# Reciprocal softmax row sums carried to all partitions by two DMAs through HBM, in an attention and expert-routing kernel on one Trainium2 core

## What is computed

```python
q = x @ Wq + bq; k = x @ Wk + bk; v = x @ Wv + bv
scores = einsum('bdsh,bdth->bdst', q, k) / SCALE
weights = softmax(scores, axis=-1)
feats = einsum('bdst,bdth->bdsh', weights, v)
x = layernorm(x + feats @ Wo + bo)
```

## Time and profile before

| | |
|---|---|
| device time, median of 3 runs | 1293.24 us (1292.84 to 1294.88) |
| span of the profiled execution | 1289.5 us |
| busy, share of the span | PE 97%, DVE 77%, ACT 71%, POOL 40% |
| attention heads | about 161 to 939 us of the span |
| granted TensorE clock | 0.999 on the mean |

### The profile page before, as it was taken

The page is one execution under the profiler, slowest core; times in us unless marked ns, Lnnn a source line. Parts: engine busy times, 40 slices in busy tenths (PEclk is TensorE's granted clock), DMA queues, the critical chain, the costliest instruction groups (busy, mean ns, idle before and its releaser), DMA issues. The chain is left out here.

```text
span 1289.5 us, 24161 instructions
## 1 busy us (share of the span) xinstructions
PE 1255.7 (97%) x8128; PEld 1058.8 (82%) x8128; DVE 998.2 (77%) x1891; ACT 919.8 (71%) x1643; POOL 513.2 (40%) x508
## 2 busy tenths in 40 slices
PE   7999999999999999999999999999988999999896
PEld 5888799889889889989989989989866877777642
DVE  5623688789889979979979979979866777776387
ACT  5421589778878868868868868878833877778343
POOL 0002223234524524524533533542543666676412
PEclk9999999999999999999999999999999999999999
DMA  8788466212424424323423423543578999997698
GB/s 282 258 283 289 155 196 223 69 42 84 147 66 138 145 70 139 125 88 110 146 84 101 155 89 88 156 136 120 178 272 326 386 386 385 346 339 252 237 426 335
DMA packets 90951, 253.14 MB, mean 196 GB/s; under 512 B 16824, under 2 KB 39480, under 8 KB 87504
## 3 DMA queue, kind: packets, MB, share of 16 engines
q1 hardware_dynamic: 70608, 196.78, 44.9%
q0 software_dynamic: 17920, 50.62, 10.2%
q10 hardware_dynamic: 2304, 4.20, 0.8%
HBM read 177.87 MB, written 134.91 MB: 243 GB/s over the span
## 5 line engine op out<-in xcount | busy, mean ns | idle before, releaser
L967 ACT ACTIVATE p_hi<-slot 128x512 fp32r<-128x512 f32 x512 | 278.5, 596 | 108.9 <-PE slot L1594 105.5
L807 POOL TENSOR_TENSOR p_lo<-prob,p_hi 128x512 fp32r<-128x512 f32 x128 | 166.1, 1297 | 441.9 <-ACT prob L969 441.7
L1607 PE MATMUL slot<-k_stack,q_stack 128*128 128x512 f32 x1024 | 300.1, 415 | 0.0
L984 ACT ACTIVATE prob<-prob,row_min 128x1024 f32<-128x1024 f32 x256 | 296.8, 1160 | 0.1
L1307 DVE TENSOR_TENSOR p_lo<-slot,p_hi 128x512 fp32r<-128x512 f32 x384 | 250.8, 681 | 52.5 <-ACT p_hi L967 51.1
L1594 PE MATMUL slot<-ident,prob 128*128 128x128 f32 x2048 | 265.8, 273 | 1.3 <-ACT prob L984 1.3
L1632 PE MATMUL pv_acc<-p_hi,v_pair 128*128 128x256 f32 x1024 | 263.1, 290 | 2.6 <-POOL p_lo L807 1.8
L1632 PE MATMUL pv_acc<-p_lo,v_pair 128*128 128x256 f32 x1024 | 253.7, 281 | 0.0
L1594 PEld LDWEIGHTS slot<-ident,prob 128*128 128x128 f32 x2048 | 229.5, 141 | 1.9 <-issue 1.7
L1632 PEld LDWEIGHTS pv_acc<-p_hi,v_pair 128*128 128x128 f32 x1024 | 192.6, 188 | 16.1 <-issue 5.7
L1632 PEld LDWEIGHTS pv_acc<-p_lo,v_pair 128*128 128x128 f32 x1024 | 192.8, 188 | 12.9 <-issue 3.3
(11 more groups left out here) (196 smaller groups left out, 1974.4 us busy)
## 6 DMA issues: line engine op xcount, KB each, us to landing
disp_hbm<-zero_hbm SPq DMA_DIRECT2D x64, 518.0 KB, 6.3
rows_all<-disp_hbm SPq DMA_DIRECT2D x64, 518.0 KB, 12.8
y_hbm<-zero_hbm SPq DMA_DIRECT2D x48, 512.0 KB, 4.4
got<-y_hbm SPq DMA_DIRECT2D x15, 1536.0 KB, 19.0
q_stack<-q_hbm SPq DMA_DIRECT2D x128, 128.0 KB, 3.1
up_pair<-in_L_ffn_w_up SPq DMA_DIRECT2D x26, 512.0 KB, 9.5
down_w<-in_L_ffn_w_down SPq DMA_DIRECT2D x32, 256.0 KB, 12.0
q_hbm<-q_hi SPq DMA_DIRECT2D x8, 512.0 KB, 2.7
```

The lines of the kernel that those rows point to most:

```text
L807: e.tensor_tensor(p_lo[1][:, 2:4, :], prob[:, m % 2, :, (4 * u + 2) * P:(4 * u + 4) * P], p_hi[1][:, 2:4, :].bitcast(F32), ALU.subtract).t ...
L967: e.activation(p_hi[b][:, two, :], view[:, two, :], ACT.Copy).then_inc(a_phi, 1)
L984: e.activation(keys, keys, ACT.Exp, bias=row_min[:, me % 2, j, 1:2], scale=-1.0, accum_out=row_sum[:, me % 2, j, half:half + 1]).then_inc( ...
L1607: made = e.matmul(slot[:, n * BANK:(n + 1) * BANK], qs[:, part, j * P:(j + 1) * P], k_stack[:, ms % H, keys], start=part == 0, stop=part == 1)
```

## The change

The two PE transposes per head and the ACT copy go, with their semaphores and the entry in the list of readers of `misc`. SP stores `row_inv` to a small HBM buffer (`store_inverse`, ahead of `load_q`), and two issue steps later loads it back to all 128 partitions of a new buffer `inv_all` (`spread_inverse`). DVE's multiply reads `inv_all` with a stride of two elements and waits for that load. Each DVE row sum waits for the store of the head before. The zeroing is regrouped: three 518 KB pieces a head instead of four, two of them between the store and the load and one behind the load; the 512 KB pieces move from the step before the load's to behind the load. The DMA scratch is set to 8192 bytes a partition.

```diff
+        inv_hbm = hbm("inv_hbm", (2, P, QT))
...
+        inv_all = sb("inv_all", [P, QC], F32, att)
...
+            def store_inverse(m):
+                e.wait_ge(v_inv, m + 1)
+                if m >= 2:
+                    e.wait_ge(d_spread, 16 * (m - 1))
+                e.dma_start(inv_hbm[m % 2], row_inv[:, :]).then_inc(d_inv, 16)
+
+            def spread_inverse(m):
+                e.wait_ge(d_inv, 16 * (m + 1))
+                if m:
+                    e.wait_ge(v_scaled, m)
+                else:
+                    e.wait_ge(v_vlo, NS)
+                    e.wait_ge(g_vlo, NS)
+                    e.wait_ge(a_vhi, 2 * NS)
+                e.dma_start(inv_all[:, :], inv_hbm[m % 2].rearrange("p j -> (p j)").partition_broadcast(P)).then_inc(
+                    d_spread, 16)
+
             jobs = []
             for s in range(LAST + LAG + 2):
+                m, u = divmod(s - LAG, STEPS)
+                if 0 <= m < NCH * H and u == 1:
+                    store_inverse(m)
+                elif 0 <= m < NCH * H and u == 3:
+                    spread_inverse(m)
                 if s < LAST and s % STEPS == STEPS - 1 and s // STEPS + 2 < NCH * H:
                     load_q(s // STEPS + 2)
...
-                elif 2 * STEPS <= s < 2 * STEPS + E - Z_EARLY:
-                    zero_disp(range(Z_EARLY + s - 2 * STEPS, Z_EARLY + s - 2 * STEPS + 1))
-                elif s % 4 == 0 and E <= s < E + 4 * NZ:
-                    e.dma_start(y_pieces[(s - E) // 4], zero_hbm[:, 0:2 * C]).then_inc(d_yzero, 16)
+                elif s >= 2 * STEPS and s % STEPS < 2:
+                    first = Z_EARLY + 3 * (s // STEPS - 2) + 2 * (s % STEPS)
+                    zero_disp(range(first, min(first + 2 - s % STEPS, E)))
+                if s % STEPS == 1 and E <= s < E + STEPS * NZ:
+                    e.dma_start(y_pieces[(s - E) // STEPS], zero_hbm[:, 0:2 * C]).then_inc(d_yzero, 16)
...
-                if 0 <= r < LAST and u == 3:
-                    e.wait_ge(p_spread, m + 1)
-                    if m:
-                        head_out(e, m - 1)
-                    e.activation(scaled[:, :], misc[:, 0:QC], ACT.Copy).then_inc(a_spread, 1)
...
-                    e.wait_ge(a_spread, mv + 1)
+                    e.wait_ge(d_spread, 16 * (mv + 1))
                     e.wait_ge(p_pv, 4 * mv + 4)
                     if mv:
                         head_out(e, mv - 1)
-                    e.tensor_tensor(scaled[:, :], pv_acc[:, 0:QC], scaled[:, :], ALU.mult).then_inc(v_scaled, 1)
+                    e.tensor_tensor(scaled[:, :].rearrange("d (j p) -> d j p", j=QT), pv_acc[:, 0:QC].rearrange("d (j p) -> d j p", j=QT),
+                                    inv_all[:, :].rearrange("d (p j) -> d j p", j=QT), ALU.mult).then_inc(v_scaled, 1)
...
                     e.wait_ge(a_exp, 4 * m + 4)
+                    if m:
+                        e.wait_ge(d_inv, 16 * m)
...
-                if 0 <= r < LAST and u == 3:
-                    e.wait_ge(v_inv, m + 1)
-                    wait_misc()
-                    for j in range(QT):
-                        made = e.transpose(misc[:, j * P:(j + 1) * P], row_inv[:, j:j + 1].to_broadcast([P, P]),
-                                           ident[:, :])
-                    made.then_inc(p_spread, 1)
-                    misc_read.append((a_spread, m + 1))
...
-    nc = _bacc.Bacc("TRN2", target_bir_lowering=False, num_devices=1)
+    nc = _bacc.Bacc("TRN2", target_bir_lowering=False, num_devices=1, dynamic_dma_scratch_size=8192)
```

More of the change, by code:

```diff
@@ L216, in build @@
         p_k, p_q, p_v = (sem(f"pe_{n}") for n in ("k", "q", "v"))
-        p_scores, p_turned, p_pv, p_spread = (sem(f"pe_{n}") for n in ("scores", "turned", "pv", "spread"))
+        p_scores, p_turned, p_pv = (sem(f"pe_{n}") for n in ("scores", "turned", "pv"))
         p_proj, p_x1t, p_gate, p_rank = (sem(f"pe_{n}") for n in ("proj", "x1_turned", "gate", "rank"))
@@ L220, in build @@
         a_xhi, a_whi, a_khi, a_qhi, a_vhi = (sem(f"act_{n}") for n in ("x_hi", "w_hi", "k_hi", "q_hi", "v_hi"))
-        a_exp, a_phi, a_copy, a_spread = (sem(f"act_{n}") for n in ("exp", "p_hi", "p_copy", "spread"))
+        a_exp, a_phi, a_copy = (sem(f"act_{n}") for n in ("exp", "p_hi", "p_copy"))
         a_x1t, a_score = sem("act_x1_turned"), sem("act_score")
@@ L238, in build @@
         d_moved, d_feats, d_st, d_st_late = (sem(f"dma_{n}") for n in ("moved", "feats", "x1_store", "x1_store_late"))
+        d_inv, d_spread = sem("dma_inverse_store"), sem("dma_inverse_spread")
         d_scat = [sem(f"dma_scatter{j}") for j in range(2)]
```

## The result

The changed kernel takes 1409.8 us (median of 4 runs, 1405.2 to 1412.6) against 1293.0 for the kernel before, 9.0% slower (ratio 1.090, 95% interval 1.0877 to 1.0923). The forecast was 1289.4 us in a range of 1280 to 1299. The profiled execution took 1412.6, its span is 1410.5, 121.0 us more than before.

The account below looks back on a forecast made before the run. The prediction took PE's instruction list to bound attention; -14.1 - 0.7 + 8.4 + 1.6 + 1.0 = -3.8 us took the span from 1289.5 to 1285.7, and the median from 1293.2 to 1289.4 us, range 1280 to 1299.

Parts of the forecast that it names:

- What the transposes cost: PE in attention: the two transposes add 0.22 us to each of 64 heads, so removing them gains 14.1 us.
- The strided multiply: DVE's multiply: taken at an unchanged 424 ns; any extra, at most 27 us in 64 heads, hidden behind DVE's idle time.
- round trip: Store and load of the reciprocals: spread lands at T + 5.4, 1.5 us inside DVE's need, costing nothing in plain heads.
- T: The end of a head's reciprocal on DVE, from which the prediction counts its times.
- The allowance: Plain heads: DVE waits for nothing if the spread lands by T + 6.93; PE stalls only from T + 8.07.
- Rival 3: Every head: the round trip is late, spread at T + 9.5, 69 us over 48 heads, 1358 us; chance 0.08.
- the main line: The forecast itself: plain heads free, chunk ends, zeroing heads and last chunk paying a little, 1289.4 us; chance 0.64.
- Chunk ends: Output projection at 7 chunk ends: feats lands late behind store and query loads, PE idle 1.2 us each, 8.4 us.
- rival 1: Chunk ends: the feats stall eats the gain, 26.5 us in 7 stalls, 1307.5 us, deciding from 1.74 us each; chance 0.13.
- The order inside the queue: DMA queue at chunk ends: feats would follow the second query load, stall about 1.5 us, sum 2.0 us worse, 1291.4.
- Zeroing heads: Heads 0 to 7: two 518 KB pieces ahead of the load make it some 0.2 us late each, 1.6 us.
- Last chunk: Residual rows and the shared expert's weights between a store and its load: at most one late head, 1.0 us.

Follow-up runs that it names:

- e14: Changed kernel with reciprocals through one SBUF partition, loaded to 64 partitions, multiplied later by POOL, query loads behind feats, chunk's first projection half a step later: 1289.7 us.
- e1: Kernel before with only the regrouped zeroing and the 8 KB DMA scratch, spread left on PE and ACT: 1292.8 us.
- e15: Changed kernel with the store's 8 B rows 64 B apart in HBM, load from 128 different rows, reciprocal values left out: 1310.1 us.
- e2: Changed kernel with the load filling inv_all from 128 different 1 KB rows of a zeroed buffer, reciprocal values left out: 1377.3 us.
- e3: As e2, and the load does not wait for the store to land; the store is still issued: 1368.1 us.
- e11: Changed kernel with e7_order's SP order; DVE copies the product without waiting, POOL multiplies by the reciprocals after the join, on 64 partitions: 1355.0 us.
- e7_order: Changed kernel with another SP order: load ahead of query loads and zeroing, feats right behind the store: 1366.9 us.
- e17_tuned: e14 with four of POOL's six chunk-end scatters half a step later and the shared expert's weights two steps later: 1286.2 us.
- e13: Changed kernel with reciprocals through one SBUF partition, loaded to 64 partitions, multiplied by POOL after the join, query loads right behind feats: 1298.0 us.
- e10: Changed kernel with the reciprocals going through one SBUF partition instead of HBM, order and waits unchanged: 1397.4 us.

## Why the prediction was wrong

**What the transposes cost: right.** 0.22 us a head was forecast; 0.21 is what unstalled heads gain (11.22 to 11.01 in e14, 15.1 to 14.9 in the changed kernel itself). The strided multiply takes 424 ns as assumed, and the scratch costs nothing (e1; the scatters wait 86.1 us where it was 87.2).

**The step that failed** is the round trip's: "its landing at T + 5.4", and from it "In plain heads the round trip costs nothing." It took 2.0 us for the store from a store of 2 KB rows and 3.1 us for the load from the query loads. Measured: 3.76 and 5.0, the load issued at T + 3.2 in the head shown and not at T + 2.35, since it now waits for the store and not for SP's list, and a landing at T + 8.5 (median). Both rows had the right direction, and the load's the right size, but another shape: the store's rows lie 8 B apart in HBM (e15), the load's 128 reads share one kilobyte (e2). The plain heads, priced at nothing, lost 33.1 us in 30 and 22.3 in the 6 last of a chunk, net of the missing transposes. The allowance was too wide as well: by the prediction PE stalls only from T + 8.07 on. In the 30 heads the spread lands at T + 8.3 (median), hardly later, but each lost 1.1 us. The prediction looked at the multiply alone; DVE's wait also holds up what PE needs of DVE, ACT and POOL afterwards: in the rows of these 30 heads PE stands 6.1 us for the multiply and 15.2 for the `p_lo` of POOL and DVE.

**Rival 3** was the case, at a chance of 0.08: its sign, DVE waiting for a DMA, shows in 46 of 64 heads, and its bounds, 4.6 and 4.8 us, were on the table. It gave 48 heads 69 us; by the table the 49 heads from the second of a chunk on lost some 64. That these agree is in part luck, since the spread landed at T + 8.5 and not T + 9.5. Its 1358 us was too low because it left zeroing heads and chunk ends at the forecast's prices. What it had in common with the main line was to take the store's harm as its own landing only. The runs showed that the transfers behind it are late too (e3, e11): `feats`, `moved` and the query loads.

**Chunk ends**: 8.4 us forecast, 25.8 measured. The mechanism was rival 1's, `feats` behind the store and the query loads: at these 7 ends it lands in 4.6 us (median; 2.6 to 6.3) and not 2.15, the longest beyond the 4.6 of the upper bound. PE stands there for 18.0 us in all, at six of the ends, 2.6 on the mean of 7, and rival 1 decides from 1.74; the multiply and the slower clock cost time there too. The order inside the queue that the prediction weighed pointed the right way, and its 1.5 us a stall were still too few. **Zeroing heads**: 1.6 us forecast, 27.0 measured in seven. With the load moved ahead of the zeroing they take 85.0 us in e7_order (summed as in the table) and not 105.6, so the order is most of it. **Last chunk**: 1.0 forecast, 10.5 measured in its last six heads; the one late head that was priced took 4.7 us of it.

**Not in the sum at all: the clock.** e17_tuned and the changed kernel issue the same 8000 PE instructions:

```profile
PE 1242.5 (97%) x8000; PEld 1045.5 (82%) x8000; DVE 1003.1 (78%) x1891; ACT 901.8 (70%) x1579; POOL 562.2 (44%) x572
```

PE is busy for 1290.8 us in the one and 1242.5 in the other, 48.3 us more for the same list, at a mean clock of 0.971 and 0.996. The spans differ by 127.7 us (1410.5 and 1282.8); the other 79.4 are idle time. So to each microsecond for which PE stood came on the mean 0.6 us more of busy time. The clock makes up at most 36 of the 48 us: 0.029 of 1410.5 us less 0.004 of 1282.8. Where the rest comes from was not tried.

Open: whether the scatters could move without making PE wait at the chunk ends, and whether rows 16 or 32 B apart with a wider load would do; neither was tried.

## What to carry to other kernels

Price a new transfer by a row of the same shape, not of the same size: here the landing hung on how many pieces went to, or came from, one place in memory, and the late store delayed the landing of what was queued behind it. Where no such row exists, take the range's far end for the plan, and ask what follows if every head pays it. A value that must travel is best used as late as the computation allows: the spread that cost 117 us at the multiply cost 63 behind the join (e11), 6 with its store in SBUF as well (e13), and with projection, scatters and weights moved too the kernel gained 6 (e17).

## What the runs showed of the hardware

- 128 stores of 8 B side by side in HBM land in 3.8 us in the changed kernel (medians of 3.0 to 4.0 in the other runs, by what stands around them), 64 B apart in 1.4 (e15), side by side in one SBUF partition in 1.9 (e10). The packets themselves are through after 1.0 us in HBM, close or apart.
- 128 reads of 1 KB from one place: out of HBM 5.0 us (3.7 from 128 places, both behind the crowded store; 2.9 behind the spaced one), out of one SBUF partition 6.4; with 64 reads out of one partition 4.2 (e17_tuned):

```profile
L663 SPq DMA_DIRECT2D inv_all<-inv_row x64: 492/548/1667, 159.9 to 928.2; - x64
...
DMA to landing us min/median/max: 3.9/4.2/6.0
```

- After PE had stood for 5.26 us the granted clock of the next 6 us was 0.59, and 8 projection matmuls took 6.05 us and not 3.67.
